# Two self-attentions of a six-stage decoder, regrouped: head-interleaved batches in the first, 128-row operands in both

## The reference

```python
def _L0_attn_ref(x, W_q, W_k, W_v, W_o):
    Q = (x @ W_q).reshape(b, s, N_HEADS, HEAD_DIM).transpose(0, 2, 1, 3)
    ...
    Qr = _apply_rope(Q, positions)
    ...
    scores = jnp.einsum('bhqd,bhkd->bhqk', Qr, Kr) / HEAD_DIM ** 0.5
    weights = jax.nn.softmax(scores, axis=-1)
    out = jnp.einsum('bhqk,bhkd->bhqd', weights, V_rep)
    ...
    return out @ W_o

def _L1_attn_ref(x, Wq, bq, Wk, bk, Wv, bv, Wo, bo, qn_w, kn_w, scale):
    ...
    q = _rmsnorm(q, qn_w)
    k = _rmsnorm(k, kn_w)
    ...
    causal = idx[:, None] < idx[None, :]
    local = jnp.abs(idx[:, None] - idx[None, :]) > WINDOW // 2
    ...
x = _layernorm(x + _L0_attn_ref(x, L0_attn_W_q, L0_attn_W_k, L0_attn_W_v, L0_attn_W_o), axis=-1)
...
x = _layernorm(x + _L1_attn_ref(x, L1_attn_Wq, L1_attn_bq, ...), axis=-1)
```

## Time and profile before

| what | value |
| --- | --- |
| timed executions | 2769.92, 2770.52, 2780.09 us; median 2770.52 |
| profiled execution | 2776.09 us, its span 2774.3 us |
| busy share of the span | PE 82%, weight loads 56%, DVE 52%, ACT 44%, POOL 33% |
| mean granted clock of PE | 0.915 of full speed |
| first attention | 0 to 591.4 us; first scores of the batches at 72.2, 206.1, 339.2, 474.6 |
| banded attention | about 845 to 1343 us |

### The profile page before, as it was taken

The page is one execution under the profiler, slowest core; times in us unless marked ns, Lnnn a source line. Parts: engine busy times, 40 slices in busy tenths (PEclk is TensorE's granted clock), DMA queues, the critical chain, the costliest instruction groups (busy, mean ns, idle before and its releaser), DMA issues. The chain is left out here.

```text
span 2774.3 us, 34127 instructions
## 1 busy us (share of the span) xinstructions
PE 2266.0 (82%) x11672; PEld 1546.3 (56%) x11672; DVE 1431.5 (52%) x2132; ACT 1209.0 (44%) x2237; POOL 904.9 (33%) x553
## 2 busy tenths in 40 slices
PE   3888888857884767768699999999999999967672
PEld 3444545426673535544477777777777777743340
DVE  1656565634554244343255575557555755543435
ACT  2636363623423434333355554555555555531312
POOL 2334242411002021120255555555555555530101
PEclk9899999988997879878899999999999999988796
DMA  2000000010001000000311121112111111130001
GB/s 101 1 1 1 1 1 1 1 50 8 1 1 44 1 1 1 1 1 1 104 44 52 45 68 45 45 45 68 45 45 45 46 45 45 45 98 1 1 1 61
DMA packets 62358, 84.01 MB, mean 30 GB/s; under 512 B 6132, under 2 KB 41332, under 8 KB 61752
## 3 DMA queue, kind: packets, MB, share of 16 engines
q1 hardware_dynamic: 62264, 82.76, 9.0%
HBM read 74.36 MB, written 4.19 MB: 28 GB/s over the span
## 5 line engine op out<-in xcount | busy, mean ns | idle before, releaser
L1859 DVE RECIPROCAL s_inv_sums<-banks 128x512 f32<-128x512 f32 x64 | 214.8, 3356 | 343.3 <-PE banks L1972 340.0
L1733 POOL TENSOR_TENSOR s_qk_rstd<-s_mean_sq,minus_half 128x8 f32<-128x8 f32 x64 | 118.5, 1852 | 500.6 <-DVE s_mean_sq L1846 500.6
L572 DVE TENSOR_REDUCE s_neg_max<-banks 128x1 f32<-128x512 f32 x256 | 170.0, 687 | 123.8 <-PE banks L633 123.6
L1965 PE MATMUL banks<-s_probsT,s_v 128*128 128x512 f32 x512 | 231.2, 594 | 0.0
L1796 ACT ACTIVATE s_probsT<-banks,s_minus_bound,s_qk_rstd 128x512 f32<-128x512 f32 x256 | 177.0, 782 | 92.6 <-PE banks L200 88.6
L529 ACT ACTIVATE s_probsT<-banks 128x512 f32<-128x512 f32 x256 | 145.4, 599 | 109.9 <-PE banks L647 109.0
L198 PE MATMUL banks<-s_w_proj_hi,xT_hi 128*128 (+1 forms) x512 | 170.2, 332 | 2.9 <-DVE s_ctxT_lo L1907 2.9
L1767 ACT ACTIVATE s_squares<-banks 128x512 f32<-128x512 f32 x64 | 38.2, 597 | 289.3 <-PE banks L200 289.3
L1965 PEld LDWEIGHTS banks<-s_probsT,s_v 128*128 128x128 f32 x512 | 97.6, 191 | 111.1 <-issue 108.5
L633 PE MATMUL banks<-s_kT,s_qT 96*128 96x512 f32 x256 | 127.3, 503 | 38.5 <-DVE s_neg_max L572 23.9
L1726 POOL TENSOR_TENSOR s_w_proj_lo<-s_w_proj_raw,s_w_proj_hi 128x2048 f32 (+1 forms) x33 | 152.1, 4610 | 13.9 <-ACT s_w_proj_hi L1759 13.9
(11 more groups left out here) (405 smaller groups left out, 5984.4 us busy)
## 6 DMA issues: line engine op xcount, KB each, us to landing
s_w_proj_raw<-l1x_wq SPq DMA_DIRECT2D x33, 512.0 KB, 4.6
s_w_out_raw<-l1x_wo SPq DMA_DIRECT2D x33, 512.0 KB, 3.9
s_w_proj_raw<-l1x_wk SPq DMA_DIRECT2D x33, 256.0 KB, 4.9
s_w_proj_raw<-l1x_wv SPq DMA_DIRECT2D x33, 256.0 KB, 5.1
x_all<-x SPq DMA_DIRECT2D x4, 1024.0 KB, 9.3
s_ctxT<-ctxT SPq DMA_DIRECT2D x8, 512.0 KB, 5.9
x_cur<-x_all SPq DMA_DIRECT2D x4, 1024.0 KB, 7.5
out<-x_all SPq DMA_DIRECT2D x4, 1024.0 KB, 4.3
```

The lines of the kernel that those rows point to most:

```text
L572: dve.tensor_reduce(nmax[:, h % 2, t, 0:1], ps.ap(s), AX.X, ALU.max, negate=True) \
L1733: pool.tensor_tensor(rs[:, j, :, :], ms[:, j, :, :], c.mhalf[:, 0:T * HP].rearrange("p (t h) -> p t h", h=HP), ALU.pow) \
L1859: dve.reciprocal(inv[:, h, :], pb.ap(("sum", h))).then_inc(pb.freed(("sum", h)), 1)
L1965: mm = pe.matmul(pb.ap(("o", h)), v[:, k, h * DX:(h + 1) * DX], probsT[:, h, k, :], start=(k == 0), stop=(k == T - 1))
```

## The change

The first attention gets the form of the banded one. A single list `seq` sets the order on all engines: for batch b, round i and tile t, the old steps of the heads, and then `extra[i, t]`, which holds parts of the next batch (X, Pq, Pk, R, C, A, H) and of the batch before (the last quotients, Y, L). ACT copies the projections into `pj` (three buffers for four tiles); DVE makes the sine half (R), POOL the cosine half (C), and DVE adds them one round later (A). The layernorm moves from DVE to ACT. The scores use all 128 rows (rows 96 and up of kT hold ones and zeros, those of qT are cleared through the bank). m shares bank 4 with X, Pq, Pk and Y; e has two banks in place of three. v is held twice. The loads of x move into this stage, in the order ident, x0, wqkv, cos_sin, x1, wo, x2, x3, and the low part of wqkv is made half by POOL and half by DVE.

```diff
+                for t in range(T):
+                    extra[0, t].append(("d", b - 1, NKV - 1, t))
+                    extra[t + 1, 1].append(("Y", b - 1, t))
+                extra[5, 3].append(("L", b - 1))
+            if b + 1 < B:
+                for k in range(KD):
+                    extra[4 + k // 2, 1 + k % 2 * 2].append(("X", b + 1, k))
+                for t in range(T):
+                    i = 7 + 2 * t if t < NPJ else 15
+                    extra[i, 1].append(("Pq", b + 1, t))
+                    extra[i + 1, 0].append(("Pk", b + 1, t))
+                    extra[i + 1, 1].append(("R", b + 1, t))
+                    extra[i + 1, 2].append(("C", b + 1, t))
+                    extra[i + 2, 1].append(("A", b + 1, t))
+                    extra[14 + t, 3].append(("H", b + 1, t))
...
+            elif s[0] in "se":
+                uses.append((s, {"s": 0, "e": 2}[s[0]] + n[s[0]] % 2, 1))
...
+            elif s[0] in ("X", "Pq", "Pk", "Y", "m"):
+                uses.append((s, 4, 1))
...
+            sp.dma_start(c.ident[:, :], d["ident"]).then_inc(first, 16)
+            load_x(0, first)
+            sp.dma_start(w, d["l0a_wqkv"].rearrange("(k p) n -> p k n", p=P)).then_inc(weights, 16)
...
+                if ph == "C":
+                    t = s[0]
+                    pool.wait_ge(*sin_done.after(b, t + 1))
+                    rope_cos(pool, pj[:, t % NPJ, :], pj[:, t % NPJ, :], cs, t).then_inc(cos_done.sem, 1)
...
+                elif ph == "e" and s[1] == 2:
+                    h = s[0]
+                    pool.wait_ge(*ps.released(0, ("e", b, h, 2)))
                     if h >= 4:
-                        pool.wait_ge(*ps.full(pos, ("o", (h - 4) // 4)))
+                        pool.wait_ge(*ps.full(0, ("o", b, (h - 4) // 4)))
...
+                elif ph == "L":
+                    pool.wait_ge(*var_ready.after(b, 1))
+                    pool.tensor_tensor(c.rstd[:, :], c.veps[:, :], c.mhalf[:, 0:T], ALU.pow).then_inc(rstd_ready.sem, 1)
...
+                elif ph == "Pq":
+                    t = s[0]
+                    act.wait_ge(*ps.full(0, ("Pq", b, t)))
+                    if t >= NPJ:
+                        act.wait_ge(*stacked.after(b, t + 1 - NPJ))
+                    act.activation(pj[:, t % NPJ, 0:D], ps.ap(("Pq", b, t)), ACT.Copy).then_inc(ps.freed(("Pq", b, t)), 1)
...
+                elif ph == "L":
+                    act.wait_ge(*nmr_ready.after(b, 1))
+                    for t in range(T):
+                        xt = c.x[:, b * T + t, :]
+                        act.activation(xt, xt, ACT.Identity, bias=nmr[:, t:t + 1], scale=c.rstd[:, t:t + 1])
...
+                elif ph == "A":
+                    t = s[0]
+                    dve.wait_ge(*sin_done.after(b, t + 1))
+                    dve.wait_ge(*cos_done.after(b, t + 1))
+                    dve.tensor_tensor(pj[:, t % NPJ, :], pj[:, t % NPJ, :], rb[:, :], ALU.add).then_inc(roped.sem, 1)
```

In the banded attention the bias rows, kT and qT go to 128 rows, the rotation is cut into N with the sine half, C and A a round apart, and X, the projections and S stand one round earlier:

```diff
-        NBR = SB + 1
-        bias = sb("bias_rows", [NBR, NQKV + D], F32R)
-        ones = sb("ones_rows", [NBR, P], F32R)
+        bias = sb("bias_rows", [P, NQKV + D], F32R)
+        ones = sb("ones_rows", [P, P], F32R)
...
-                    extra[2 + k].append(("X", b + 1, k))
-                extra[14].append(("S", b + 1))
+                    extra[1 + k].append(("X", b + 1, k))
                 for t in range(T):
-                    extra[6 + 2 * t].append(("Pq", b + 1, t))
-                    extra[7 + 2 * t].append(("Pk", b + 1, t))
-                    extra[14 + t].append(("R", b + 1, t))
+                    extra[5 + 2 * t].append(("Pq", b + 1, t))
+                    extra[6 + 2 * t].append(("Pk", b + 1, t))
+                extra[13].append(("S", b + 1))
+                for t in range(T):
                     extra[15 + t].append(("H", b + 1, t))
+                for t in range(T):
+                    extra[13 + t] += [("N", b + 1, t), ("C", b + 1, t)]
+                for t in range(T):
+                    extra[14 + t].append(("A", b + 1, t))
```

More of the change, by code:

```diff
@@ L414, in rope_attention, with cnt @@
-        steps = [s for s in steps if s[:2] != ("d", NKV - 1)]
+        nmr = sb("ln_minus_mean_rstd", [P, T])
+        w = probsT[:, 0:3, :, :].rearrange("p a b c -> p (a b c)")[:, 0:KD * NQKV].rearrange("p (k n) -> p k n", k=KD)
+        def cnt(name, per=1):
+            return Count(c.sem("s1_" + name), per)
+        first, weights, table = c.sem("s1_first_x_loaded"), c.sem("s1_weights_loaded"), c.sem("s1_table_loaded")
+        wo_in = c.sem("s1_wo_loaded")
+        x_in = [None] + [c.sem(f"s1_x{b}_loaded") for b in range(1, B)]
@@ L415, in rope_attention @@
+        seq += [("d", B - 1, NKV - 1, t) for t in range(T)] + [("Y", B - 1, t) for t in range(T)] + [("L", B - 1)]
         uses = []
         n = {"s": 0, "e": 0}
[L417 to L418 removed]
+        for s in seq:
+            if s[0] == "q":
                 uses.append((s, 5, 1))
[L420 to L427 removed]
@@ L436, in rope_attention @@
+        ps.open(uses)
         block = ctx.enter_context(nc.Block())
@@ L483, in _, with turned_hi @@
-            act.activation(wq_hi[:, :, :], wraw, ACT.Copy).then_inc(w_hi, 1)
-            def project(b, pos, heads_before):
-                c.act_x_hi(act, b, pos)
-                for t in range(T):
+            def turned_hi(b, k):
+                act.wait_ge(*ps.full(0, ("X", b, k)))
+                act.activation(c.xhi[:, k, :], ps.ap(("X", b, k)), ACT.Copy).then_inc(x_hi.sem, 1)
+            for k in range(KD):
+                turned_hi(0, k)
+            act.wait_ge(weights, 16)
+            act.activation(w_h[:, :, :], w, ACT.Copy).then_inc(w_hi, 1)
@@ L497, in project @@
                     act.activation(ks[:, t, :, 2 * HD:].bitcast(F32R), rk, ACT.Copy).then_inc(r_hi.sem, 1)
-            def keys(b, pos, heads_before):
-                act.wait_ge(*r_hi.after(b, T))
-                if heads_before is not None:
-                    act.wait_ge(*ps.full(heads_before, ("o", NKV - 1)))
-                act.activation(v[:, :, :], v_next[:, :, :], ACT.Copy).then_inc(v_out.sem, 1)
-                for g in range(NKV):
-                    act.wait_ge(*ps.full(pos, ("k", g)))
-                    act.activation(kT[0:STK, g, :], ps.ap(("k", g))[0:STK, :], ACT.Copy) \
-                       .then_inc(ps.freed(("k", g)), 1)
@@ L577, in last_quotients, with turned_lo @@
-            def last_quotients(pos):
-                for t in range(T):
-                    quotient(pos, NKV - 1, t)
-            def output(b, pos):
-                if pos is LAST_OUTPUT:
-                    last_quotients(at("heads", pos[0]))
-                c.dve_layernorm(dve, b, pos)
-            turns(dve, project, nothing, heads, output)
+            def turned_lo(b, k):
+                dve.wait_ge(*x_hi.after(b, k + 1))
+                dve.tensor_tensor(c.xlo[:, k, :], ps.ap(("X", b, k)), c.xhi[:, k, :].bitcast(F32), ALU.subtract) \
+                   .then_inc(ps.freed(("X", b, k)), 1)
@@ L670, in output, with turned @@
-            def output(b, pos):
-                pe.wait_ge(*ps.released(at("heads", pos[0]), ("o", NKV - 1)))
-                for t in range(T):
-                    ps.wait_empty(pe, pos, ("y", t))
+            pe.wait_ge(first, 32)
+            def turned(key, rows, source):
+                ps.wait_empty(pe, 0, key)
+                for t in range(T):
+                    mm = pe.transpose(ps.ap(key)[0:rows, t * P:(t + 1) * P], source(t), c.ident[:, :])
+                mm.then_inc(ps.filled(key), 1)
@@ L674, in output @@
                     for k in range(KD):
-                        mm = pe.matmul(ps.ap(("y", t)), outT[:, k, t * P:(t + 1) * P], wo[:, k, :],
+                        mm = pe.matmul(ps.ap(key), outT[:, k, t * P:(t + 1) * P], wo[:, k, :],
                                        start=(k == 0), stop=(k == KD - 1))
-                    mm.then_inc(ps.filled(("y", t)), 1)
-            turns(pe, project, keys, heads, output)
-        ps.close(B)
-        for count in (c.xT_hi, c.var_ready, c.rstd_ready):
-            count.close(B)
@@ L713, in nothing @@
+        ps.close(1)
 def nothing(*_):
@@ L1215, in window_attention @@
         seq += [("S", 0)]
-        for t in range(T):
-            seq += [("R", 0, t), ("H", 0, t)]
+        for t in range(T + 2):
+            seq += [("H", 0, t - 2)] if t > 1 else []
+            seq += [("N", 0, t), ("C", 0, t)] if t < T else []
+            seq += [("A", 0, t - 1)] if 0 < t <= T else []
         for b in range(B):
```

511 lines of the change are left out of this document (273 added, 238 removed).

## The result

The changed kernel takes 2877.34 us (four runs, 2877.20 to 2881.53) against 2774.2 (four runs) of the kernel before: a ratio of 1.0372, 95% interval 1.035 to 1.0394. It is slower by 103 us. The forecast was 2833, so the measured time is 44 us above it: inside the range 2745 to 2885, near its upper end, but outside the forecast's own 2797 to 2868 and where rival C (2870 and over) begins.

A forecast was written before the change was run, and what follows sets the result against it. PE was taken as busiest, a plain round not PE-bound. Batches +101, start -18, clock +6 made +89; with banded attention and bias products -26, +63 on 2776.1 gave 2839, less 5.6: 2833. Range 2745 to 2885, own 2797 to 2868.

The forecast's parts named there:

- rival C: First attention: two waits per batch bring following stretches to the lower clock, another 35 us and more: 2870 and over; chance 0.10.
- Additive rounds: First attention's heads: work put between heads adds to a 3.69 us round, its 0.9 us open time absorbing none.
- Rival A: First attention: rounds take up their open 0.9 us and stalls fall into existing waits, a batch 118, time 2697; chance 0.08.
- The three stalls: PE stands 6.1 us at DVE's sum, 7.2 at the layernorm in round 5; in the tail the fourth projection's copy waits.
- a POOL that could pass its waiting addition: First attention: POOL makes the cosine half first, stalls at DVE's sum vanish, 18 us less, 2815; a tenth of the forecast's chance.
- The tail of batch 1: From the complete third group to the next scores: remaining additions, stacks, quotients and keys on in-order engines take 32.2 us.
- Start: Before batch 0: earlier loads and a halved low part bring the first projection to 21.5 from 41.07: -18 us.
- the bias products: Projections and outputs: 48 products at 128 rows save some 0.29 us each, -14, of which 2 fall into waits: -12.
- the banded attention: Second stage: earlier rotation chain -12 at three changes, first batch -4, bias products -12, memset +1.7, X beside Y +1: about -26.
- the clock, "+6": First attention: PE stands more, so the mean granted clock falls 0.02 on half of 600 us: +6 us.
- rounds 8 to the third group: Batches 1 and 2: 44.8 before, 14 for projections, 6.1 for DVE's sum, 3.4 for bank 4 waits: 68.3 us.
- The 3.4 us a batch: Round 8 to the third group: waits for bank 4, about 0.9 before each of four Pk.

The follow-up runs named there:

- the version with both edits and the output in one piece: Changed kernel with cosine half ahead of POOL's waiting addition, layernorm split over rounds, last quotients and output projection together before the key transposes: 2788.2 us, ratio 1.005.
- the cosine edit: Changed kernel with the cosine half moved up on POOL, ahead of the addition that waits for a complete group: 2828.6 us, ratio 1.0209.
- the experiment: Changed kernel with the turned maxima back on the bank of the q transposes, all else the same: 2847.6 us, ratio 1.0265.

## Why the prediction was right or wrong

*Additive rounds: right, and it carried the sign.* In the version with both edits and the output in one piece, rounds 4 to 14 of batch 1 take 21.3 us more than before (79.1 against 57.8), for 5 of X and three projections of 4.2, 17.6: nothing of it was hidden. Y in its rounds cost 7.95 - 3.63 = 4.3 for 3.5 of work, and 3.7 with the maxima on their own bank. Rival A, that a round takes up its open 0.9 us, falls. (Its 2697 was also summed wrongly: three batches at 118 are the 48 us, and the start's 18 are not in it.)

*The three stalls: right in place and chain.* 7.16, 6.58 and 5.82 us, each named ahead, each gone when its order was changed. The order on POOL is what makes them; a POOL that could pass its waiting addition, priced at 18 us, is what the cosine edit imitates, and it gave 49. The tail of batch 1 took 32.0 us where 32.2 were forecast, but that is in part luck: PE was busy 17.9 us in it at a granted clock of 0.73, and a part of the fourth projection is in it, both of which the forecast had put elsewhere.

*Start, and the bias products: right.* -18.0 for -18, and 14.8 us for the 48 products, against 14 before the deduction of 2. The rule that a product's height does not matter does not hold for these; the trace was the better guide. In the banded attention -24.9 for -26: the 15 us gap did not shorten, but the shorter gaps behind it fell from 23.8 to 10.2 us in sum, near the 12 that were forecast for the three changes; the first batch's gap shortened by 2.6, not 4.

*Mis-sized, the main one: the clock, "+6".* The first attention came out 37 us longer than forecast (+125.9 for +89). Between its first scores and its end PE stands 106 us more than before (178.1 against 72.1), where the batches were forecast at +101. PE's busy time rose from 452.4 to 490.3 us for the same products, 38 us, where the clock had +6. So 32 of the 37 us are clock. The granted clock of the batches was 0.83 to 0.88 (full and half level mixed) against 0.92 to 0.96, a drop of about 0.09 and not 0.02. The stretches at the half level lie at the gaps: the gap of 7.16 us ended at 316.81, and from 312.5 to 322.5 the granted clock was 0.50, after 1.00 in the stretch of dense work before it (302.7 to 309.6). This is rival C's mechanism, beside the forecast's, and C's time of 2870 and over is where the kernel came out.

*Mis-sized: DVE beside POOL, in rounds 8 to the third group, 68.3 forecast and 77.4 measured.* The step "Only then can DVE make A (about 0.9 ...)" took the duration from an instruction that reads a bank. The changed rotation reads pj and the table, both in SBUF, and beside POOL's work A took 1.8 us and the sine half 2.3 to 2.6. That gave 1 us more in round 11 and the two gaps of 3.9 and 3.7 after the sine half that no term held. POOL and DVE were priced as if alone. The Trainium skill, page "SBUF — State Buffer", section "SBUF: two separate sides", says that a DVE operation with two SBUF inputs and a GpSimd operation that reads SBUF exclude each other for the whole instruction. The traces agree: 480 to 514 ns for the sine half with POOL's additions cut, up to 1547 with them. Of the 9.1 us some 6 are PE's busy time (58.5 against 38.7 of before and 14 of projections, an estimate) and some 3 standing. That all standing together came to 106 for 101 although these two gaps, 7.6 us a batch, were not in it is in part luck: other terms must have been too large, and the runs do not say which.

*Mis-sized: bank 4.* The 3.4 us a batch that I gave it left out X and Y; the experiment measured 26 us over the stage, 18 of standing and 8 of PE's busy time.

The three overlap, since gaps of the second and third kind also cost clock, and cannot be added up to the 37 us.

## What to carry to other kernels

Before work is put between heads, look at what a round with foreign work cost in the trace at hand: if it is added, interleaving can only win what the gap it fills was losing, and here that gap was 12 us a batch. Price new gaps twice, as standing and as clock: here 106 us of standing came with 38 us of longer busy time. On in-order engines each moved instruction must be checked for what stands ahead of it and waits longest; one place further up on POOL was worth 49 us. And an instruction that is moved from a bank to SBUF operands must be priced beside what POOL does at that time.

## What the runs showed of the hardware that I had not expected

- DVE's product of two SBUF tensors of 128x320: 0.48 us, and up to 1.55 us while POOL adds. The sum of 128x640: 0.82, and 1.80.
- A product of 33 rows among products of 128 rows costs 0.31 us more of PE's time than one of 128 rows (48 of them, 14.8 us); one of 96 rows among scores showed no such cost at the full clock (0.319 against 0.316 to the next).
- ACT's four passes of 0.8 us in a row, with POOL's addition and the power ahead of them, cost a round 7.1 us; one in each of four rounds cost nothing that shows.
